# Moving the row normalization of two layer norms to ScalarE and turning the last two feed-forward groups together

## What is computed

```
qkv = x @ Wqkv + bqkv ; qp, kp = elu(q)+1, elu(k)+1
attn = qp @ (kp^T v) / (qp @ sum(kp) + 1e-6)
x = layer_norm(x + attn, g1, b1)
ffn = (silu(x @ Wg + bg) * (x @ Wu + bu)) @ Wd + bd       # 682 hidden units
return layer_norm(x + ffn, g2, b2)
layer_norm(x, g, b) = (x - mean) * rsqrt(var + 1e-5) * g + b
```

## Time and profile before

| | |
|---|---|
| median of 3 runs | 1093.75 us (1093.63 to 1093.96) |
| the profiled execution | 1092.6 us |
| its span, first to last instruction | 1090.8 us |
| mean granted clock of TensorE | 0.91 of full speed |
| TensorE busy / VectorE / ScalarE / GpSimd | 908.2 / 766.1 / 377.2 / 414.7 us |
| linear attention from its output tail | about 395 to 427 us |
| feed-forward stage | about 427 to 573 us |

### The profile page before, as it was taken

The page is one execution under the profiler, slowest core; times in us unless marked ns, Lnnn a source line. Parts: engine busy times, 40 slices in busy tenths (PEclk is TensorE's granted clock), DMA queues, the critical chain, the costliest instruction groups (busy, mean ns, idle before and its releaser), DMA issues. The chain is left out here.

```text
span 1090.8 us, 17828 instructions
## 1 busy us (share of the span) xinstructions
PE 908.2 (83%) x5603; PEld 771.2 (71%) x5612; DVE 766.1 (70%) x1473; ACT 377.2 (35%) x709; POOL 414.7 (38%) x480
## 2 busy tenths in 40 slices
PE   3499999999657864988856788877679999999998
PEld 1499999999646653867755655436368888888887
DVE  5788888888458798588655656435557777677776
ACT  4366556665134212122214155455511111111110
POOL 3177877778500340544317322300022323233232
PEclk9599999999979876999977799897789999999999
DMA  8336122341160001400008700000011010000002
GB/s 270 104 121 194 48 68 96 116 163 51 45 200 1 0 1 42 145 1 1 1 0 145 156 1 1 1 1 1 1 30 30 14 29 23 20 29 14 29 0 78
DMA packets 50300, 61.81 MB, mean 57 GB/s; under 512 B 8014, under 2 KB 37768, under 8 KB 50248
## 3 DMA queue, kind: packets, MB, share of 16 engines
q1 hardware_dynamic: 43464, 43.85, 13.0%
q0 software_dynamic: 6336, 17.31, 6.6%
q10 hardware_dynamic: 448, 0.01, 0.0%
HBM read 47.26 MB, written 7.60 MB: 50 GB/s over the span
## 5 line engine op out<-in xcount | busy, mean ns | idle before, releaser
L2248 POOL TENSOR_TENSOR e_hl<-e_h32sb,e_hh 128x512 fp32r<-128x512 f32 x68 | 88.1, 1296 | 289.9 <-DVE e_hh L2272 289.9
L2239 ACT ACTIVATE e_silusb<-psum 128x512 f32<-128x512 f32 x68 | 40.7, 598 | 242.2 <-PE psum L2192 242.2
L2280 DVE SCALAR_TENSOR_TENSOR y<-psum,comb,y 128x256 f32<-128x256 f32 x272 | 112.2, 476 | 0.1
L2269 DVE TENSOR_TENSOR e_h32sb<-psum,e_silusb 128x512 f32<-128x512 f32 x68 | 47.0, 692 | 84.6 <-PE psum L2192 71.3
L443 ACT ACTIVATE e_u<-psum,e_bias 128x256 f32<-128x256 f32 x152 | 63.7, 471 | 96.3 <-PE psum L342 87.5
L2192 PE MATMUL psum<-act_hi,e_w0h 128*128 128x512 f32 x144 | 58.0, 403 | 9.8 <-ACTq L2232 9.8
L1274 POOL TENSOR_TENSOR ff_hl<-ff_h32sb,ff_hh 128x512 fp32r<-128x512 f32 x24 | 34.5, 1439 | 71.1 <-DVE ff_hh L1309 71.1
L1836 DVE TENSOR_REDUCE at_mn<-psum 128x4 f32<-128x512 f32 x64 | 42.3, 687 | 24.7 <-PE psum L1533 18.8
L2192 PE MATMUL psum<-act_hi,e_w0l 128*128 128x512 f32 x144 | 57.2, 397 | 0.0
L2192 PE MATMUL psum<-act_lo,e_w0h 128*128 128x512 f32 x144 | 57.1, 397 | 0.0
L352 PE MATMUL psum<-e_w3h,e_h2h 128*128 (+1 forms) x160 | 47.1, 295 | 8.6 <-issue 8.2
(11 more groups left out here) (503 smaller groups left out, 3228.2 us busy)
## 6 DMA issues: line engine op xcount, KB each, us to landing
e_raw<-in_W SPq DMA_DIRECT2D x16, 512.0 KB, 7.0
e_raw<-in_W SPq DMA_DIRECT2D x8, 1024.0 KB, 5.8
y<-in_x SPq DMA_DIRECT2D x4, 512.0 KB, 9.8
v_tok<-in_xT SPq DMA_DIRECT2D x4, 512.0 KB, 8.2
y<-y_rows SPq DMA_DIRECT2D x4, 512.0 KB, 6.9
v_tok<-y_rows SPq DMA_DIRECT2D x4, 512.0 KB, 7.8
v_tok<-in_x SPq DMA_DIRECT2D x4, 512.0 KB, 8.7
e_raw<-in_w_gate SPq DMA_DIRECT2D x16, 128.0 KB, 2.2
```

The source lines that it names most:

```text
L2239: act.activation(sl_sb[:, s % 2, :], ps[s % 2][:, :], ACT.Silu).then_inc(sil, 1)
L2248: pool.tensor_tensor(hh[1][:, s % HS, :], h32[:, s % 2, :], hh[0][:, s % HS, :], ALU.subtract).then_inc(hsp, 1)
L2269: dve.tensor_tensor(h32[:, s % 2, :], ps[2 + s % 2][:, :], sl_sb[:, s % 2, :], ALU.mult).then_inc(h32d, 1)
L2280: dve.scalar_tensor_tensor(out=y[:, i, :], in0=ps[4 + j][:, 0:D], scalar=comb[:, i, bass.ds(2 * t + out_s // G, 1)], in1=y[:, i, :], op0=A ...
```

## The change

Both layer norms now compute x * rstd + shift with shift = -mean * rstd. VectorE makes the reciprocal and the 128x4 shifts (`shift_group`); ScalarE applies both per row as scale and bias of an Identity activation, four per group (`norm_group`); VectorE or GpSimd goes on with gain and bias once `scaled` is set. Besides: in linear attention `norm(2)` (now its shift alone) stands one output earlier, after output 12, and its gain where the whole was. In the feed-forward stage ScalarE's four activations stand after the silu of m = 4, and VectorE's gain moves from m = 4 to m = 5, behind the last slice of the group. In the last group TensorE runs down(3) ahead of turn(2), then turn(2) and turn(3), and VectorE's low parts of group 2 follow `add(3)`.

```diff
@@ stage_linear_attention, scalar, for g in range(G)
                         act.activation(rstd[...], rstd[...], ACT.Sqrt).then_inc(root, 1)
+                        norm_group(act, y, g, rstd, shift, shifted, scaled)
                         if g >= OL - 1 and g + 1 < G:
@@ vector
                     def norm(g):
-                        norm_group(ch, y, g, mv, rstd, root, g + 1)
-                        if g < OL:
-                            dve.nop().then_inc(scaled, 1)
-                        else:
-                            gain_group(ch, y, g, gb[:, 0, :], group_rows(gb[:, 1, :])).then_inc(normed[1], 1)
+                        shift_group(ch, g, mv, rstd, shift, root, shifted)
+
+                    def gain(g):
+                        dve.wait_ge(scaled, g + 1)
+                        gain_group(ch, y, g, gb[:, 0, :], group_rows(gb[:, 1, :])).then_inc(normed[1], 1)
...
+                        if i == NB + TG:
+                            norm(OL)
                         if i == NB + TG + 1:
-                            norm(OL)
+                            gain(OL)
                     for g in range(OL + 1, G):
                         norm(g)
+                        gain(g)
@@ helpers
-        def norm_group(ch, src, g, mv, rstd, root, n_root):
+        def shift_group(ch, g, mv, rstd, shift, root, shifted):
             dve = ch.eng
             sl = slice(g * TG, (g + 1) * TG)
-            dve.wait_ge(root, n_root)
+            dve.wait_ge(root, g + 1)
             ch.link(dve.reciprocal(rstd[:, sl], rstd[:, sl]))
+            dve.scalar_tensor_tensor(out=shift[:, sl], in0=mv[:, sl, 0], scalar=-1.0, in1=rstd[:, sl],
+                                     op0=ALU.mult, op1=ALU.mult).then_inc(shifted, 1)
+        def norm_group(act, src, g, rstd, shift, shifted, scaled):
+            act.wait_ge(shifted, g + 1)
             for i in range(g * TG, (g + 1) * TG):
-                last = dve.tensor_scalar(src[:, i, :], src[:, i, :], mv[:, i, 0:1], rstd[:, i:i + 1],
-                                         ALU.subtract, ALU.mult)
-            ch.link(last)
+                last = act.activation(src[:, i, :], src[:, i, :], ACT.Identity, scale=rstd[:, i:i + 1], bias=shift[:, i:i + 1])
+            last.then_inc(scaled, 1)
@@ stage_feed_forward, tensor
                         if g + 1 < G:
                             up((g + 1) * FC)
-                        if g:
-                            turn(g - 1)
+                            if g:
+                                turn(g - 1)
                         down(g)
-                    turn(G - 1)
+                    for g in range(G - 2, G):
+                        turn(g)
@@ scalar
+                        if g and m == 4:
+                            norm_group(act, y, g - 1, rstd, shift, shifted, scaled)
...
                     hi(G - 2)
                     take_root(G - 1)
+                    norm_group(act, y, G - 1, rstd, shift, shifted, scaled)
                     hi(G - 1)
@@ vector
                         if g and m == 3:
-                            norm_group(ch, y, g - 1, mv, rstd, root, g)
-                        if g and m == 4:
+                            norm(g - 1)
+                        if g and m == FC - 1:
                             gain(g - 1)
...
+                    add(G - 1)
                     lo(G - 2)
-                    add(G - 1)
-                    norm_group(ch, y, G - 1, mv, rstd, root, G)
+                    norm(G - 1)
                     gain(G - 1)
```

More of the change, by code:

```diff
@@ L755, in stage_linear_attention @@
             kvps, kvdone, nps, nuse = sem("la_kvps"), sem("la_kvdone"), sem("la_nps"), sem("la_nuse")
-            rreq, root, densum, scaled, gained = (sem(f"la_{x}") for x in ("rreq", "root", "densum", "scaled", "gained"))
+            rreq, root, densum, shifted, scaled, gained = (sem(f"la_{x}") for x in ("rreq", "root", "densum", "shifted", "scaled", "gained"))
             normed = [sem(f"la_normed{n}") for n in range(2)]
@@ L771, in stage_linear_attention @@
                 stats, mv, rstd = sbl("la_stats", [P, NT, 6]), sbl("la_mv", [P, NT, 2]), sbl("la_rstd", [P, NT])
+                shift = sbl("la_shift", [P, NT])
                 block = st.enter_context(nc.Block())
@@ L1139, in stage_feed_forward @@
             ops, used, rreq, root, normed = (sem(f"ff_{x}") for x in ("ops", "used", "rreq", "root", "normed"))
+            shifted, scaled = sem("ff_shifted"), sem("ff_scaled")
             mask_in = [sem(f"ff_mask{n}") for n in range(2)]
@@ L1155, in stage_feed_forward @@
                 mv, rstd = small[:, 6 * NT:8 * NT].rearrange("p (i s) -> p i s", s=2), small[:, 8 * NT:9 * NT]
+                shift = small[:, 9 * NT + QT * QT:10 * NT + QT * QT]
                 block = st.enter_context(nc.Block())
@@ L1338, in count, with norm @@
                                           .rearrange("p (j t) -> p j t", t=P), AX.X, ALU.add)
+                    def norm(g):
+                        shift_group(ch, g, mv, rstd, shift, root, shifted)
                     def gain(g):
+                        dve.wait_ge(scaled, g + 1)
                         dve.wait_ge(xbiased, g + 1)
```

## The result

The changed kernel takes 1080.72 us (median of 4 runs, 1078.88 to 1082.82) against 1093.69 us of the kernel before, measured with it: ratio 0.9887, 95% interval 0.9861 to 0.9913. The forecast was 1088.9 us with a range of 1086.0 to 1091.8; the direction was right, the size was not: 13 us came where 4.8 were forecast.

The account below looks back on a forecast made before the run. VectorE was taken to bound linear attention's tail, and TensorE alternating with VectorE, GpSimd and turn the feed-forward. Savings of 1.7 and 3.1 us, summed as 4.8, gave 1087.8 us profiled, 1088.9 against the median; range 1086.0 to 1091.8.

Parts of the forecast that it names:

- Linear attention: Linear-attention stage: VectorE back at the outputs 2.5 us earlier, norm(2) -0.1, norm(3) +0.9, sum -1.7 us.
- The first rival: Both norms: small shift not held by GpSimd, or activations as short as 1.69 us; total 1087.0 us, chance 18%.
- The pieces of feed-forward: Feed-forward stage: savings of 0.2, 0.8 and 3.85 us in groups 1 to 3, less 1.75 in the tail: 3.1 us.
- Tail: Feed-forward after down(3): turn(2), root's table load, low parts and dearer round trip make the last gain 1.75 us later.
- Failed step 1: Feed-forward group 1: low clock in TensorE's idle time, eight transposes 1.97 us instead of 1.09, down(1) 0.6 us longer.
- Failed step 2: Between stages: a barrier passes an earlier stage's saving on unchanged, so untouched stages were forecast to change by 0 us.
- Linear attention saves nothing: Rival, linear attention: something outside VectorE, GpSimd or the low clock, sets its tail; total 1090.6 us, chance 10%.
- The round trip is exposed everywhere: Slower rival, both norms: eight round trips at 0.9 us cost 7.2, less 3.85 saved; total 1097.1 us, chance 4%.
- GpSimd comes last: Rival, feed-forward group 3: GpSimd's last low part follows both gain halves, losing 2.4 of 3.85 us; 1091.3 us, chance 15%.
- Low clock: Slower rival, feed-forward: a further quarter of each down at low clock costs 2.6 us each; total 1096.7 us, chance 3%.

Follow-up runs that it names:

- after_again: The changed kernel run once more with no edit, for a second profile: 1083.48 us.
- la_only: Against the changed kernel, feed-forward put back as before, so only linear attention is changed: 1094.52 us, ratio 1.0008 to the kernel before.
- order_only: The kernel before with only the last group's order changed, down(3) ahead of turn(2): 1089.12 us, ratio 0.9958.
- before_again: The kernel before run once more with no edit, for a second profile: 1095.04 us.
- after: The changed kernel's first run and profile: 1080.72 us, ratio 0.9887 to the kernel before.
- turns_last: slices_first with, in every group, the product ahead of the turn of the group before: 1069.28 us, ratio 0.9777 to the kernel before.
- slices_first: roots_first with ScalarE's feed-forward scaling after the silu of slice 5 and GpSimd's b2 addition behind slice 5: 1072.99 us, ratio 0.9812 to the kernel before.
- roots_first: The changed kernel with both square roots of linear attention's groups 0 and 1 ahead of ScalarE's first scaling: 1081.11 us, ratio 0.9882 to the kernel before.
- norms_only: The changed kernel with the last group's old order, turn(2), down(3), turn(3): 1085.64 us, ratio 0.9925 to the kernel before.

## Why the prediction was wrong

**Linear attention: right in the stage, with luck.** Forecast -1.7, measured -1.65. The last gain ends 111.1 to 111.4 us into the stage in six of the seven profiles with this change, 112.8 to 113.1 in the eight with the old stage. In the seventh, after_again, it ends at 113.15 and nothing is saved: L743 was held by GpSimd. The prediction had no term for that meeting, which the change brought about and which went well by 0.02 us or less. The shift of group 1 waited for GpSimd, the gains waited for ScalarE 1.16 and 2.14 us. The rule cited from the Trainium skill ("SBUF — State Buffer", "Who interferes with whom"), that two SBUF inputs contend with GpSimd's reads, agrees with the trace at this small size too: 128x4, 2.19 us beside GpSimd and 0.16 us alone. The first rival (shift not held, or activations of 1.69 us) fell with it. But the stage's 1.7 us did not reach the end when it stood alone (la_only, 1.0008).

**The pieces of feed-forward: right in the main.** Four activations 2.07 us (2.05), gain 0.1 us earlier (0.3), no wait for GpSimd ahead of down(1) and down(2), GpSimd's part between the two halves of the gain. Down(3) starts 19.38 us after the end of down(2) instead of 23.11: 3.73 us (3.85). Tail +1.70 us (+1.75). order_only shows that the moved product earns this only together with the scalings on ScalarE: alone it starts down(3) no earlier. The table in the Trainium skill ("ScalarE: Activation LUTs", "Rules for kernel authors"), which gives a bf16 rate as its reason, speaks against such a move; for these float32 tiles the trace agrees with it for the instructions where VectorE has them to itself (2.07 against 1.38 us) and not beside GpSimd (4.44 and 5.45 us).

**Failed step 1, feed-forward: "I expect the low clock (1.2 GHz, granted 0.5) there", and the lengths of the products that were taken from it.** turn(0) was priced at 1.97 us and down(1) as 0.6 us longer, down(2) and down(3) as unchanged. Measured: from the end of one down to the start of the next 21.40 and 21.91 us instead of 23.15 and 23.16, so 1.75 and 1.25 us saved where 0.8 each was forecast; lengths of down(1) to down(3) 10.03, 9.52, 10.40 against 10.06, 10.68, 10.83, so 1.6 us less, not 0.6 more. With 0.6 us lost at the stage's head the sum is -6.0. The four other profiles in which turn(0) and turn(1) did take 1.97 us part the two: there the turns' price was right (1.0 us saved in each group, in the place of 0.8), and the products' lengths were still wrong (down(1) 9.35 to 10.19 us where 10.7 was forecast); after_again's stage is 4.8 us shorter than before_again's, after's 6.05 shorter than before's. What the sum had wrong in all of them is that the low stretches would be as long as before or longer: from the end of down(0) to that of down(3) they came to 23.9 us before, 13.7 in after and 17.1 in after_again. That the low stretches shrink further with the idle time before a down is what turns_last adds (none between the head of the stage and the last us before down(3)); why they do was not isolated.

**Failed step 2, the larger one: "what an earlier stage saves moves all that follows by the same amount."** 5.3 us came in attention and conditioning. The barrier does pass a saving on, but the stage behind it has its own low stretches, and whether they come depends on where it starts relative to the clock's rises. Waits alone reproduce it in both directions. It cuts the other way in la_only, where the 1.8 us saved were lost again in feed-forward. In the sum this term was zero, with no bound of either sign: it should have been in the range. Which part of the 1.7 us in conditioning follows attention's and which has its own place was not separated; it moved with attention in most profiles (64.2 where attention took over 157 us, 61.0 to 62.6 in the others), but slices_first has 61.04 and roots_first 62.38 with the same attention (153.4).

**The rivals.** *Linear attention saves nothing* holds in one profile of seven, for the reason above. *The round trip is exposed everywhere* is out (it gave 1097.1 us). *GpSimd comes last* is out (its last low part ran between the halves of the gain, 2.17 us as before). *Low clock* was a rival of the slow side only; the clock moved the other way.

## What to carry to other kernels

Where a profile shows the granted clock at its low level in several stages, a change of one microsecond can, as here, be worth five or minus seven further on. Before crediting an edit, compare stages that it does not touch, and run the kernel with two or three short waits in front of the next stage: if its time does not follow the wait, the gain is one of place, and it can go with the next edit. Work that is taken off an engine helps only what waits for it: 3.2 us of VectorE's time per group went to ScalarE, and the gain ended 0.1 us earlier. Putting the slices that a product needs ahead of work that it does not need took 6.3 us more off the feed-forward stage (slices_first), and running the products ahead of the turns another 4.8 (turns_last). And where a change lets two engines meet that did not meet before, read the starts of both: here the order of two instructions 0.02 us apart is worth 1.9 us.

## What was not expected of the hardware

- An untouched stage of 157 us took 153.4 to 157.6 us, sorted by the distance from its start to the clock's next rise (2.9 to 5.9 us): 157.25 to 157.61 us at 2.9 to 3.3, 153.35 to 153.98 at 3.7 to 4.7, 154.7 to 155.5 at 5.0 to 5.9. norms_only stands next to the jump of 4 us, and its single runs spread over 8.5 us.
- Waiting 1.3 us longer made the kernel before 0.35% faster.
- A 128x4 instruction of VectorE with two SBUF inputs took 2.19 us beside GpSimd, as much as a large one. A 128x4 `tensor_scalar` with one tensor input took 2.37 us when it started 0.008 us behind GpSimd's addition, and 0.17 us when it started between 0.017 us ahead and 0.005 us behind.
